# Two woven attentions in one Trainium2 kernel: a step of four tanh becomes two steps of two, each with its own place in the order

## The reference, cut to what matters

```python
# layer 2 attention (additive part): tanh of every query-key pair, summed over the features with weights W2
hid = jnp.tanh(hq[:, :, None, :] + hk[:, None, :, :] + b1)
est = jnp.einsum('bqkh,h->bqk', hid, W2[0]) + b2[0]
attn = jax.nn.softmax(scores + est, axis=-1)
...
# layer 3 attention, for each of 8 heads
dot = jnp.where(causal[None, None], jnp.einsum('bhtd,bhsd->bhts', q, kk_), -jnp.inf)
attn = jax.nn.softmax(dot, axis=-1)
out = jnp.einsum('bhts,bhsd->bhtd', attn, v)
```

## Time and profile before

| what | value |
|---|---|
| median of three executions | 4598.27 us |
| profiled execution: its time | 4594.98 us |
| profiled execution: its span, first to last instruction | 4593.1 us |
| PE busy, ACT busy, DVE busy over the span | 91%, 63%, 61% |
| the three woven stretches of tanh | first tanh at 3273.6, 3654.0 and 4032.2 us |
| matmuls, ACT instructions | 25119, 6125 |

### The profile page before, as it was taken

How to read it: one execution, slowest core, us unless ns; L and a number is a source line. 1 busy time by engine, 2 the same in 40 slices (tenths; PEclk the granted TensorE clock), 3 DMA queues, 4 the chain that set the end, 5 groups by cost and what they waited for, 6 DMA issues and landing times.

```text
span 4593.1 us, 67780 instructions
## 1 busy us (share of the span) xinstructions
PE 4165.6 (91%) x25119; PEld 2334.1 (51%) x25119; DVE 2788.3 (61%) x6459; ACT 2872.6 (63%) x6125; POOL 692.7 (15%) x466
## 2 busy tenths in 40 slices
PE   6788779999999999999999999968888888997988
PEld 4454434444444444444444444434556655665666
DVE  5655567777777777777777777622343344245254
ACT  1222247877787877778777777765664474474533
POOL 0000112222222222222222222100000000000000
PEclk9877779999999999999999999979999999999999
DMA  2000034333342424242433424000100000100000
GB/s 108 1 28 0 21 45 53 46 46 55 41 69 37 57 43 53 50 53 44 52 50 53 57 36 59 24 31 24 36 1 19 26 1 10 31 1 1 28 4 4
DMA packets 94423, 160.53 MB, mean 35 GB/s; under 512 B 18272, under 2 KB 75024, under 8 KB 93712
## 3 DMA queue, kind: packets, MB, share of 16 engines
q1 hardware_dynamic: 94096, 156.20, 20.4%
HBM read 74.04 MB, written 7.82 MB: 18 GB/s over the span
## 4 chain that ended last, share of the span: by engine, by line
PE 74%; DVE 9%; issue 6%; ACT 6%; DVEq 2%; PEld 1%; POOL 1%; DMA 1%; PEldq 0%; POOLq 0%; SPq 0%; ACTq 0%
PE ps L1151 12%; PE ps L1187 12%; PE ps L1161 10%; PE ps L1507 9%; PE ps L1221 4%; PE ps L1230 4%; PE ps L1142 2%; PE ps L1038 2%; PE ps L1639 2%; PE ps L1250 2%; PE ps L1439 2%; DVE peaks L2225 2%; PE ps L1601 1%; PE ps L1577 1%; PE ps L1023 1%
## 5 line engine op out<-in xcount | busy, mean ns | idle before, releaser
L2225 DVE TENSOR_REDUCE peaks<-ps 128x1 f32<-128x748 f32 (+1 forms) x1536 | 1408.4, 933 | 481.8 <-PE ps L1161 459.6
L1796 ACT ACTIVATE masked<-ps 128x384 f32<-128x384 f32 (+3 forms) x1536 | 683.1, 486 | 197.2 <-PE ps L1151 185.0
L1796 ACT ACTIVATE probs<-ps 128x384 f32<-128x384 f32 (+1 forms) x1536 | 662.3, 484 | 74.1 <-PE ps L1151 73.6
L912 POOL TENSOR_TENSOR rstd<-var,minus_half 128x6 f32<-128x6 f32 x104 | 138.3, 1329 | 2875.2 <-DVE var L2458 1484.5
L1151 PE MATMUL ps<-shared 98*128 98x384 bf16 (+3 forms) x1536 | 447.3, 327 | 4.4 <-ACT probs L1796 1.7
L1151 PE MATMUL ps<-q_stack,k_stack 98*128 98x384 bf16 (+3 forms) x1536 | 449.9, 328 | 0.9
L1161 PE MATMUL ps<-k_stack,q_stack 96*128 96x374 bf16 (+1 forms) x1536 | 380.7, 329 | 37.0 <-DMA k_stack<-parts 21.5
L1161 PE MATMUL ps<-shared 96*128 96x374 bf16 (+1 forms) x1536 | 372.1, 323 | 8.7 <-DVE peaks L2225 8.0
L1151 PEld LDWEIGHTS ps<-shared 98*128 98x128 bf16 (+1 forms) x1536 | 147.9, 103 | 336.6 <-ACT masked L1796 125.9
L1151 PEld LDWEIGHTS ps<-q_stack,k_stack 98*128 98x128 bf16 (+1 forms) x1536 | 149.7, 103 | 328.4 <-ACT masked L1796 121.2
L1161 PEld LDWEIGHTS ps<-k_stack,q_stack 96*128 96x128 bf16 (+1 forms) x1536 | 154.6, 105 | 159.4 <-DVE peaks L2225 44.3
(11 more groups left out here) (571 smaller groups left out, 7684.6 us busy)
## 6 DMA issues: line engine op xcount, KB each, us to landing
shared<-parts SPq DMA_DIRECT2D x192, 187.0 KB, 9.2
wr<-in_l SPq DMA_DIRECT2D x32, 580.5 KB, 3.5
q_stack<-parts SPq DMA_DIRECT2D x96, 187.0 KB, 7.8
k_stack<-parts SPq DMA_DIRECT2D x96, 187.0 KB, 10.3
wts<-in_l SPq DMA_DIRECT2D x32, 514.5 KB, 3.6
wrow<-in_l_rows SPq DMA_DIRECT2D x32, 320.0 KB, 4.1
wq<-in_l SPq DMA_DIRECT2D x32, 192.0 KB, 3.3
const<-in_const SPq DMA_DIRECT2D x1, 4202.5 KB, 12.9
```

The source lines that it names most:

```text
L912: pool.tensor_tensor(lane.rstd, lane.var, minus_half[:, :], ALU.pow).then_inc(S["rstd_ready"], 1)
L1796: act.activation(probs_ring(u)[0:m, 0:hi - lo], src[0:m, 0:hi - lo], ACT.Exp, scale=float(HD) ** -0.5).then_inc(S["ring_done"], 1)
L2225: v.tensor_reduce(peaks[0:m, g, j, head:head + 1], src[0:m, :, 0:T // 2], XY, ALU.max)\
```

## The change

Part 0's list gets two steps in place of each `("add", u, q)` for the tiles 0 to 5: `("add", u, q)` at a cost of 2.1 and `("more", u, q)` at a cost of 1.85, in place of one at 3.95, so that the total stays. On ACT `add` issues the first two tanh of the quad and `more` the other one or two, raises `hidden_ready`, and has the exponentials in front of its tanh for q = 1. PE and DVE do nothing at `more`; their work stays at `add`, whose middle lies 0.925 cost units earlier than before.

```diff
-        steps += [(("add", u, q), 3.95) for u in range(NT) for q in range(4)]
+        steps += [step for u in range(NT) for q in range(4)
+                  for step in ((("add", u, q), 2.1), (("more", u, q), 1.85))]
...
-                def add(lane, k, u, q):
-                    if u == 0 and q == 0:
+                def add(lane, k, u, q, more=False):
+                    if u == 0 and q == 0 and not more:
...
-                    if q == 0 and u < 2:
+                    if q == 0 and u < 2 and not more:
...
-                    if quad and s >= TANH_SLOTS:
+                    if quad and s >= TANH_SLOTS and not more:
...
-                    for i, (g, _) in enumerate(quad):
+                    first, end = (2, len(quad)) if more else (0, 2)
+                    for i, (g, _) in list(enumerate(quad))[first:end]:
                         if q == 1 and u and i == 2:
                             exponentials(lane, k)
...
-                    if quad:
+                    if quad and more:
                         last.then_inc(S["hidden_ready"], 1)
-                    elif q == 1:
+                    elif q == 1 and not quad:
                         exponentials(lane, k)
...
-                    elif what == "add":
-                        add(lane, k, *at)
+                    elif what in ("add", "more"):
+                        add(lane, k, *at, what == "more")
```

## The result

The changed kernel took 4640.66 us (median of 4 executions, 4640.02 to 4642.33) against 4598.06 us before (4 executions). The kernel before, timed again beside the experiments, spread from 4589.3 to 4602.9 in 25 executions. The ratio is 1.0093, with a 95% interval of 1.0075 to 1.011. The forecast was 4620, range 4592 to 4640: the sign and the mechanism held, the size did not, and the measured time lies just outside the range.

The account below looks back on a forecast made before the run. PE, busy 91%, was taken to be bound by lock-step in the woven stages, its standing still counting. Terms gave +12.4 us a stage, taken as +7.5; three stages, +22.5 on 4598.3, gave 4620.8, say 4620 (range 4592 to 4640).

Parts of the forecast that it names:

- What gets dearer: PE's new waits for second halves of twelve quads in each woven stage: 19.4 us a stage.
- What gets cheaper: PE's waits in a woven stage that go or shorten: 6.2 us for ACT, at most 1.9 for DVE.
- The wait of 3.38: PE's wait for last 39's copy, behind quad (4, 1) and the exponentials: 2.4 us less, down to about 1.
- quad (0, 2): PE's wait for this quad around last 12: 1.95 us before, near 1.6 after, 0.35 gone.
- 1.9 at most: Of PE's 2.6 us of waits for DVE in a stage, at most 1.9 fall away as the additive maximum comes earlier.
- The sum: Per woven stage: +19.4 + 1.1 - 6.2 - 1.9 = +12.4 us, then taken as +7.5 because waits are not independent.
- The walk: Going through a stage's new list in order with estimated durations: about +5.5 us, or +8 with what it neglects.
- The clock: PE's granted clock behind new waits: bounds none to 7 us a stage, taken near the lower end.
- the two low stretches of before: PE at a clock of 0.57 and 0.66 behind the waits of 1.95 and 3.38, 1.7 us each, in every stage.
- the third rival: Waits come in full and pull the clock down: 15 to 18 us a stage, 4643 to 4652 us; chance 0.10.
- Finer grain wins: Rival: waits for second halves stay under the savings and stages shorten; 4564 us at best, more likely 4587; chance 0.12.
- The order hardly matters: Rival: a wait that goes reappears at the next meeting of the two batches; 4598 us within 9; chance 0.13.

Follow-up runs that it names:

- the far quads: Changed kernel with only quads (u, 0) and (u, 1) of tiles 1 to 5 split, the others whole at the first half's place: 4572.94 us.
- whole late quads: Changed kernel with no quad split: ACT does each whole at the second half's place, PE and DVE stay early: 4768.02 us.

## Why the prediction was wrong, point by point

**What gets dearer: right, wait by wait.** The sum was 19.4 us a stage over twelve quads; the rows above add up to 20.7, or 20.3 without quad (0, 0). Quads (u, 0) and (u, 1) of the later tiles did stay early, but the reason given, that both are consumed two steps on, holds for (u, 0) only; (u, 1) is covered by PE's own work ahead of it, as shown with the far quads. `products` waits about as before (3.0 for 3.5).

**What gets cheaper: right in kind.** The wait of 3.38 became 0.9, last 8's and last 45's went, quad (0, 2) went from 1.95 to 1.24. Last 32 waits 0.9 for its copy, 1.1 forecast. Not forecast is that last 26 now waits 1.34 for a value's copy. The waits for DVE stayed, 2.8 before and 2.6 after, so that the "1.9 at most" gave 0.2.

**The sum: this is the step that failed.** The terms gave +12.4 a stage. The prediction then said "But the waits are not independent", walked the list through in order, came out at +5.5 to +8, and took +7.5. Measured are +14.3 of standing still. There is no discount. The walk had 8 us at the end of tile 3 and only 4 after last 40; by the first matmul of `products` in the two traces, tile 3 was 8.2 us late (3366.4 for 3358.2), tile 4, right behind last 40, 10.2 (3397.8 for 3387.6) and tile 5 12.9 (3426.1 for 3413.2), although the stage had begun 1.2 us earlier. It never fell back. Two quads made whole took away 15.8 us of waits and 14.5 of standing still; one quad split added 7.5 of waits and 7.3 of standing still. Where PE is the busiest of three engines in lock-step, at 88% in the stages of before, a new wait was paid nearly in full. That this is so because PE has to do later what it misses then fits the runs, but none of them varies how full PE is.

The +12.4 itself is near the 14.3 partly by luck. It holds a slip: quad (0, 2) waits 1.95 before, so its new wait of 1.6 is no addition, and the sum counts it as one beside the 0.35 that it saves. Without the slip the terms give +10.8. What they lack of 14.3 is mainly the DVE waits that did not go (1.7), last 26's wait (1.3) and the quads' waits being 1.3 longer than forecast in all, against 0.5 less at the exponentials.

**The clock: a smaller part of the error.** The forecast charged nothing for it, near the lower end of its own bounds of 0 to 7 us. PE's busy time rose by 1.9 a stage, all of it in the second stage, where the same matmuls took 6.3 us more. Of the 8.6 a stage by which 16.1 is over 7.5, the standing still has 6.8 and this 1.9. (The walk had PE at full clock throughout. If it thereby also took the two low stretches of before, 3.4 us a stage, for gone, that much of the 6.8 belongs to the clock; its text does not say. That the lateness it let fall by 4 us after last 40 did not fall holds either way.) With +12.4 and "one or two low stretches more" the third rival had 15 to 18 a stage, 4643 to 4652; measured are 16.1 a stage and 4640.7, between its range and mine. Its mechanism, the waits in full, was the right one, and it was given 0.10. The rule of the Trainium skill (TensorE: Matmul & The Clock Gate, section "A second HAM failure mode: psum-queue depth-cycling"), that frequent short idles make the clock oscillate, agrees in direction: 5.6 us more of PE's busy time in three stages with the change, 55 with whole late quads, 9 less with only the far quads split.

**The rivals.** Finer grain wins: not as changed, but its idea was sound where the consumer is far. With the quads of q 0 and 1 of the tiles 1 to 5 alone the same edit is 24 us faster than before, 8 to 11 of them from the early place. The order hardly matters: refuted, the change cost 42.6 us where that rival allowed 9, and the orders tried run from 4569 to 4768 us with the same work.

## What to carry to other kernels

When a producer's step is split in two and its consumer keeps its place, what shrinks is the distance from the end of the product to its use. List for each consumer what the second half now stands behind, and split only where the consumer has enough to do ahead of its use to outlast the second half (a whole step more, or work of its own in the same step): that choice was worth 71 us here, between 4640.7 and 4569.5. In this kernel, where the engine that waits was the one closest to full, the right price was the sum of the new waits less the old ones, with no discount for catching up. Count a wait that only changes its length by the difference, and add something for the clock.

## What the runs showed of the hardware

The same wait was followed by a stretch at the low clock in one place and not in another. In the first stage the wait of 2.55 us ahead of quad (0, 3) was followed by a clock of 1.00, in the second stage the same wait ahead of the same matmuls, here in the timeline of PE, by 0.57 for 4 us.

```profile
3692.52 2.10 PE L1441 MATMUL ps<-hid,add_w 128*32 128x374 f32 x12 [2.55 <-ACT hid L1963]
```

Of the five waits for tanh of 1.95 us and more in the changed kernel's first stage, two were followed by 1.00 (2.46 and 2.55) and three by 0.57 to 0.59 (2.72, 2.12 and 1.97). One length of a wait does not tell.

Outside the woven stages, where all kernels have the same instructions in the same order, the span varied from 4006 to 4020 us between profiled executions. Single executions of one kernel spread as widely (the kernel before from 4589.3 to 4602.9). So some differences of under 10 us between these kernels can't be put down to a stage. Its cause stays open.
